# The last step of a Mamba scan on VectorE and ScalarE: states not stored, three factors multiplied at once

## What is computed

```python
def step(h, inp):                       # h: batch x 512 channels x 16 states
    d_t, u_t, B_t, C_t = inp
    dA = jnp.exp(d_t[..., None] * A)
    h = dA * h + (d_t * u_t)[..., None] * B_t[:, None, :]
    y = jnp.einsum('bdn,bn->bd', h, C_t)
    return (h, y)
_, ys = jax.lax.scan(step, h0, (deltas, us, Bs, Cs))
y = (ys + us * D[None, None, :]) * _silu(zs)
out = jnp.einsum('md,lbd->lbm', out_proj_w, y)
```

## Time and profile before

| what | us |
|---|---|
| runs: median (lowest to highest of 3) | 541.82 (541.18 to 544.04) |
| the profiled execution, its span | 540.9 |
| busy in the span: TensorE / VectorE / ScalarE / GpSimd | 437.8 / 399.3 / 314.3 / 216.1 |
| last scan step on VectorE, first product to last gate | 229.79 to 253.85 |
| first attention projection starts | 255.05 |

### The profile page before, as it was taken

One profiled execution on the slowest core, in us unless ns is written; L12 is line 12 of the kernel. 1 busy time (PEld: TensorE's weight loads), 2 busy tenths in 40 slices (PEclk: granted clock), 3 DMA queues, 4 the chain that ended last, 5 costly groups with the idle time before them and its releaser, 6 DMA issues.

```text
span 540.9 us, 9798 instructions
## 1 busy us (share of the span) xinstructions
PE 437.8 (81%) x3248; PEld 360.2 (67%) x3248; DVE 399.3 (74%) x734; ACT 314.3 (58%) x728; POOL 216.1 (40%) x157
## 2 busy tenths in 40 slices
PE   4979931848688685868999999999999999998733
PEld 1435621727577474756888988888988888897512
DVE  1867699796999999996564677776767777677453
ACT  2646995686999988986143453534355353435310
POOL 2300009793978979780323222223222223323010
PEclk9989975787896979889999999999999999999865
DMA  8952538031110223123000000000000000000000
GB/s 291 362 221 79 161 99 268 26 92 47 50 39 21 70 67 118 53 74 123 19 1 1 11 2 21 0 0 19 0 19 0 19 0 0 19 0 21 0 10 10
DMA packets 18795, 32.92 MB, mean 61 GB/s; under 512 B 2129, under 2 KB 11729, under 8 KB 17937
## 3 DMA queue, kind: packets, MB, share of 16 engines
q1 hardware_dynamic: 18768, 32.59, 18.1%
HBM read 26.26 MB, written 6.32 MB: 60 GB/s over the span
## 4 chain that ended last, share of the span: by engine, by line
PE 40%; issue 19%; ACT 15%; DVE 14%; DMA 6%; POOL 4%; SPq 1%; DVEq 0%; POOLq 0%; ACTq 0%
PE ps L398 32%; PE ps L505 5%; DMA ud_t<-ud_dram 4%; ACT hc L831 4%; ACT ps L823 2%; DVE reg_b L1227 2%; POOL reg_b L1056 2%; PE ps L602 2%; ACT reg_b L806 2%; ACT reg_b L918 1%; POOL small L1038 1%; DVE ps L1220 1%; DVE reg_b L1118 1%; DVE reg_b L1280 1%; DMA Nw<-x_fm 1%
## 5 line engine op out<-in xcount | busy, mean ns | idle before, releaser
L1033 POOL TENSOR_TENSOR reg_b<-reg_c,reg_a 128x1024 f32<-128x1024 f32 x56 | 130.5, 2372 | 60.7 <-DVE reg_c L1170 60.4
L1056 POOL TENSOR_TENSOR reg_b<-reg_b 128x768 f32<-128x768 f32 x32 | 58.0, 1812 | 140.1 <-DVE reg_b L1280 107.5
L398 PE MATMUL ps<-x1T,Mw 128*128 (+1 forms) x768 | 93.6, 278 | 0.6 <-ACT Mw L884 0.6
L831 ACT ACTIVATE hc<-reg_b,bc 128x512 f32<-128x512 f32 x112 | 79.8, 713 | 21.6 <-PE ps L505 18.3
L398 PEld LDWEIGHTS ps<-x1T,Mw 128*128 128x128 f32 x768 | 88.2, 192 | 4.3 <-ACT Mw L884 0.9
L505 PE MATMUL ps<-ident,hc 128*128 128x128 f32 x452 | 75.9, 318 | 15.3 <-ACT hc L831 15.1
L1227 DVE SCALAR_TENSOR_TENSOR reg_b<-reg_c,bc,ps 128x512 f32<-128x512 f32 x112 | 81.9, 736 | 0.0
L505 PEld LDWEIGHTS ps<-ident,hc 128*128 128x128 f32 x452 | 62.0, 165 | 26.2 <-ACT hc L831 25.1
L1220 DVE TENSOR_TENSOR ps<-ps,reg_b 128x512 f32<-128x512 f32 x96 | 65.8, 690 | 7.6 <-ACT ps L823 7.5
L823 ACT ACTIVATE ps<-reg_b 128x512 f32<-128x512 f32 x112 | 65.5, 586 | 4.1 <-POOL reg_b L1033 4.1
L918 ACT ACTIVATE reg_b<-ps,small 128x128 f32<-128x128 f32 x128 | 45.3, 366 | 38.8 <-DVE small L1285 38.2
(11 more groups left out here) (138 smaller groups left out, 705.8 us busy)
## 6 DMA issues: line engine op xcount, KB each, us to landing
reg_a<-a_dram SPq DMA_DIRECT2D x4, 1024.0 KB, 8.0
Mw<-w_o SPq DMA_DIRECT2D x1, 2048.0 KB, 15.9
ud_dram<-reg_b SPq DMA_DIRECT2D x4, 512.0 KB, 3.8
zs_dram<-x1T SPq DMA_DIRECT2D x4, 512.0 KB, 3.7
mring<-w_q SPq DMA_DIRECT2D x8, 256.0 KB, 2.9
ud_t<-ud_dram SPq DMA_DIRECT2D x8, 256.0 KB, 3.3
zs_t<-zs_dram SPq DMA_DIRECT2D x8, 256.0 KB, 2.7
Nw<-zeros SPq DMA_DIRECT2D x1, 2048.0 KB, 9.8
```

The costliest lines, as they stand in the source:

```text
L398: return pe.matmul(o, l, r, start=start, stop=stop)
L831: act.activation(hc[:, (n + 1) % WRING, :], H[:, n, :], ACT.Copy, scale=bc[:, t, s:s + 1]).then_inc(hc_s, 1)
L1033: pool.tensor_tensor(dA[:, g % RING], delta_r[:, bass.ds(t, 1), :].to_broadcast([P, SA, DI]), Abc[:, g * SA:(g + 1) * SA, :], ALU.mult).th ...
L1056: pool.tensor_tensor(rq[:, g % 2].rearrange("p a c n -> p (a c n)"), pc[:, g % 2].rearrange("p a c n -> p (a c n)"), psn[:, g % 2].rearran ...
```

## The change

In step 7 no state is stored, since no later step reads one. As y is the sum over n of C * (dA * h + B * du), it is split: the sum of C*B is one scalar per row (cb_last, made in the first part), and du times that scalar is added to ud_t, so that it comes onto Y with the skip row; what is left of each state is dA * C * h, one VectorE instruction that reads the exponential in PSUM, C as a scalar and the old state, and writes hc. ScalarE weighs nothing in step 7. The step is written out as `last_step`: it first waits for ud_t's load. The loop runs over steps 2 to 6. In `last_step` gate(6) stands after state 3, norm1_stats(6) after state 10 and norm1(6) after state 13. Two semaphores are new: udl_s (ud_t is complete) and yl_s (a product is written), and the sum takes small[:, 18:19]. The diff without the declarations:

```diff
--- before.py
+++ after.py
@@ -508,14 +508,17 @@
             def skip_sum(t):
 
                 need(pe, y2_s, t)
-                pe.wait_ge(st_u, 16 * (t + 1))
+                if t == T - 1:
+                    pe.wait_ge(udl_s, 1)
+                else:
+                    pe.wait_ge(st_u, 16 * (t + 1))
                 for c in range(CI):
                     last = turn_onto(Y[:, c * P:(c + 1) * P], ud_t[:, c * P:(c + 1) * P], c == 0, False)
                 last.then_inc(udm, 1)
 
-            def state_sum(slot, count, last_state):
-
-                pe.wait_ge(hc_s, count)
+            def state_sum(slot, done, count, last_state):
+
+                pe.wait_ge(done, count)
                 for c in range(CI):
                     last = turn_onto(Y[:, c * P:(c + 1) * P], hc[:, slot, c * P:(c + 1) * P], False, last_state)
                 last.then_inc(y_s, 1)
@@ -539,12 +542,15 @@
                 last.then_inc(x1Tm, 1)
 
             skip_sum(0)
-            state_sum(0, 1, True)
+            state_sum(0, hc_s, 1, True)
             pe.wait_ge(ld["wout"], 16)
             for t in range(1, T):
                 skip_sum(t)
                 for n in range(NST):
-                    state_sum((n + 1) % WRING, NST * (t - 1) + n + 2, n == NST - 1)
+                    if t == T - 1:
+                        state_sum((n + 1) % WRING, yl_s, n + 1, n == NST - 1)
+                    else:
+                        state_sum((n + 1) % WRING, hc_s, NST * (t - 1) + n + 2, n == NST - 1)
                     if n in PE_SIDE:
                         side_job(per_step * (t - 1) + PE_SIDE.index(n))
                     if n == 3:
@@ -815,7 +821,10 @@
 
 
                 act.wait_ge(arg_s, AG * (t - 1) + n // SA + 1)
-                need(act, h_s, NST * (t - 1) + n + 1 - RING)
+                if t == T - 1 and n >= RING:
+                    act.wait_ge(yl_s, n + 1 - RING)
+                else:
+                    need(act, h_s, NST * (t - 1) + n + 1 - RING)
                 if t == 1 and n == 0:
                     act.wait_ge(act_free, freed[("Z", CI - 1)][1])
                 if t == 1 and n == 2:
@@ -888,9 +897,9 @@
             def scan_step(t, carried):
                 for n in range(NST):
                     decay(t, n)
-                    if n >= BEHIND:
+                    if n >= BEHIND and t < T - 1:
                         weigh(t, n - BEHIND)
-                    elif carried:
+                    elif n < BEHIND and carried:
                         weigh(t - 1, NST + n - BEHIND)
                     if n in ACT_SIDE:
                         take_side(per_step * (t - 1) + ACT_SIDE.index(n))
@@ -900,8 +909,6 @@
 
             for t in range(1, T):
                 scan_step(t, t > 1)
-            for n in range(BEHIND):
-                weigh(T - 1, NST + n - BEHIND)
             for j in range(len(side) - sum(n >= NST for n in ACT_SIDE), len(side)):
                 take_side(j)
             take_x1(T - 1)
@@ -1194,7 +1201,11 @@
             softplus(1)
             dve.wait_ge(cb_s, 1)
             dve.tensor_reduce(cb0, cb_n[:, :], AX.X, ALU.add).then_inc(cb_s, 1)
+            dve.wait_ge(cb_s, 2)
+            dve.tensor_tensor(cb_n[:, :], bc[:, T - 1, 0:NST], bc[:, T - 1, NST:2 * NST], ALU.mult).then_inc(cb_s, 1)
             step_inputs(0)
+            dve.wait_ge(cb_s, 3)
+            dve.tensor_reduce(cb_last, cb_n[:, :], AX.X, ALU.add).then_inc(cb_s, 1)
             softplus(2)
             step_inputs(1)
             softplus(3)
@@ -1268,9 +1279,30 @@
                     elif n == 11:
                         norm1(t - 1)
 
+            def last_step():
+
+                t = T - 1
+                dve.wait_ge(st_u, 16 * T)
+                dve.wait_ge(cb_s, 4)
+                dve.scalar_tensor_tensor(ud_t[:, :], du_r[:, t, :], cb_last, ud_t[:, :], ALU.mult,
+                                         ALU.add).then_inc(udl_s, 1)
+                for n in range(NST):
+                    dve.wait_ge(da_s, NST * (t - 1) + n + 1)
+                    dve.wait_ge(y_s, NST * (t - 1) + n + 2 - WRING)
+                    dve.scalar_tensor_tensor(hc[:, (n + 1) % WRING, :], ps[:, n % RING, :],
+                                             bc[:, t, NST + n:NST + n + 1], H[:, n, :], ALU.mult,
+                                             ALU.mult).then_inc(yl_s, 1)
+                    if n == 3:
+                        gate(t - 1)
+                    elif n == 10:
+                        norm1_stats(t - 1)
+                    elif n == 13:
+                        norm1(t - 1)
+
             scan_step(1)
-            with dve.Fori(2, T) as t:
+            with dve.Fori(2, T - 1) as t:
                 scan_step(t)
+            last_step()
 
             def rope(k, g):
                 dve.wait_ge(xa_s, k + 1)
```

More of the change, by code:

```diff
@@ L123, in decoder_layer @@
         stats2, aggr2 = small[:, 48:54], small[:, 54:56]
-        cb0 = small[:, 62:63]
+        cb0, cb_last = small[:, 62:63], small[:, 18:19]
         spare = small[:, 63:64]
@@ L211, in decoder_layer @@
         arg_s = sem("arg_s"); da_s = sem("da_s"); dah_s = sem("dah_s"); h_s = sem("h_s")
-        cb_s = sem("cb_s"); hc_s = sem("hc_s"); y_s = sem("y_s"); udm = sem("udm")
+        cb_s = sem("cb_s"); hc_s = sem("hc_s"); yl_s = sem("yl_s"); udl_s = sem("udl_s"); y_s = sem("y_s"); udm = sem("udm")
         st_x = sem("st_x"); st_z = sem("st_z"); st_u = sem("st_u")
```

## The result

| kernel | median, us | lowest to highest | ratio to before (95% interval) |
|---|---|---|---|
| before | 541.82 | 541.0 to 544.04 (5 runs) | |
| changed | 545.49 | 544.55 to 546.17 (5 runs) | 1.0061 (1.0041 to 1.0081) |
| changed, once more beside the later experiments | 545.54 | 543.66 to 547.07 (12 runs) | 1.0059 (1.0038 to 1.0081) |

Times in us are read from medians; whether a kernel is faster or slower is read from the ratio.

The account below looks back on a forecast made before the run. The prediction took step 7's end to hang on ud_t's late load, then TensorE up to the first attention projection. +3.96 (gate) + 0.59 (clock) - 1.38 (lighter VectorE) = +3.2 us, from 541.82 to 545.0, range 542.3 to 546.8.

Parts of the forecast that it names:

- The wait at the head: Start of step 7: VectorE stands about 7.5 us until ud_t lands; ScalarE stands too after four exponentials.
- The gate behind it: Step 7: gate(6) follows ud_t's wait and four states, so TensorE starts the skip sum 3.96 us later.
- The slow clock: Skip sum to state 4 on TensorE: 6.42 us instead of 5.83 after longer idle time, +0.59 us.
- step 2's row: Same piece, skip sum to state 4, in scan step 2 before the change: 6.42 us after 8.51 us idle.
- The tail: State 4 to the last side job in step 7: 9.1 us against 10.48 with lighter VectorE work, -1.38 us.
- A state's price: Step 7 on VectorE: the one remaining instruction per state costs 0.65 us of queue, bounds 0.605 and 0.736.
- The beginning: First part, between the softplus parts: two small added instructions fall into VectorE's waits and cost nothing; uncovered, about 0.3 us.
- Behind the scan: After step 7: the rope tables' load goes out later, with 6.7 us left before use; costed at nothing.
- What bounds the kernel before: Step 7: ud_t's late load, then TensorE up to the first attention projection at 255.05; VectorE's queue alone doesn't decide.
- TensorE alone in the tail: Rival, from state 4 on: norm1(6) is ready in time, tail 7.5 us, total +1.6 or +1.0; chance 0.17.
- second slow stretch: Rival, before turn_x1(6): TensorE's new idle time slows its clock again, total +4.5 us, 546.3; chance 0.12.
- VectorE's queue as the limit: Rival, step 7: VectorE's queue and not the gate's place decides, -2.9 us, 538.9; chance 0.05.

Follow-up runs that it names:

- wait-only kernel: Kernel before with step 7 written out behind the loop on VectorE and a wait for ud_t's load at its head, arithmetic unchanged: 547.75 us, ratio 1.0102.
- The experiment with the gate first: Changed kernel with gate(6) moved to the head of last_step, ahead of the wait for ud_t: 541.92 us, ratio to before 1.000.
- kept-busy run: Changed kernel with 64 unused transposes of ident on TensorE ahead of skip_sum(7): 543.58 us, ratio to before 1.0027.

## Why the prediction was right, point by point

Forecast 545.0, measured 545.49; the sum was +3.2, the medians differ by 3.7 and the traces by 3.20 at the first projection, counted from ud_t's issue (in the profile's own time it starts at 256.35 and not at 258.2, because the issue itself came 1.90 sooner). The mechanism was right as well, in the order forecast. That the sum and the traces agree so closely is luck, since the terms are off by up to 0.18 us and cancel; of the 0.5 by which the medians go beyond the traces, 0.2 lies outside the span and the rest stays open.

- *The wait at the head.* VectorE idle 7.5 us expected, 7.21 seen; in the wait-only kernel 7.31. ScalarE did stand behind it, for 6.22 us, as said.
- *The gate behind it.* +3.96 expected, +3.78 seen; ud_t came 0.26 us quicker after its issue (3.34 us to VectorE's first instruction, 3.60 to TensorE's in the earlier trace rows), and the addition, four states and the gate took 4.04 instead of 3.96. TensorE's idle time 8.26 for 8.44. The experiment with the gate first shows that the gate's place behind the wait is the cause of the loss.
- *The slow clock.* +0.59 expected from step 2's row, +0.66 seen. It is the least certain term, and that it came so near is luck: the same kernel gave 5.98 instead of 6.49 in its second profile. Step 2's row was taken since its idle time was nearest, and this ground doesn't hold: by the table above 3.29 us idle led to 7.06, beyond the bound of 6.71 that I gave, and 10.53 to 6.12. The Trainium skill (TensorE: Matmul & The Clock Gate, Part 1) says that activity releases the throttle of an idle array. The kept-busy run agrees with it: the clock was 1.00 from 234 to 245.
- *The tail.* -1.38 expected, -1.24 seen (9.24 for 9.1). The wait for x1 was 1.11 for 1.3, and norm1's place its cause.
- *A state's price.* 0.65 us of queue expected for the new instruction: four take 2.72 at a duration of 0.75 each, that is 0.66 between starts.
- *The beginning.* Nothing expected. From the reduction of cb_n to the instruction that waits for ScalarE it is 5.40 us in both kernels (59.25 to 64.65, 61.22 to 66.62 in the earlier trace rows): the two instructions lie inside the waits. *Behind the scan.* The tables had the 6.7 us foreseen (252.69 to 259.40), and the wait ahead of L1311 was TensorE's, as before.
- *What bounds the kernel before.* The prediction followed TensorE from ud_t on and said that VectorE's queue alone doesn't tell when the step ends. The two experiments on the kernel before show that it does, but for 0.45 us: 23.61 us from first product to last gate, whether ud_t comes early or is waited for at the head, against 24.06. This didn't hurt the sum: its terms started from measured stretches, and that VectorE's queue makes TensorE's tail of 10.48 longer than it need be was reckoned with in the last of them.
- *Not foreseen.* GpSimd, of which I said that it runs ahead and isn't late, was itself stopped for 2.99 us by the exponentials; nobody waited for it. And the kernel before with the wait alone was expected at +7.5 and came at +6.3 by the medians, +6.8 in the trace: I counted all of the wait, though 0.45 us of it is made good behind it in this step. The 0.5 between the trace and the medians stays open.

Of the rivals, TensorE alone in the tail was refuted by the wait of 1.11 us; no second slow stretch came (the clock was 1.00 from 244 on). VectorE's queue as the limit is refuted for the changed kernel, where VectorE waits for TensorE, and shown for the kernel before, where the earlier transfer brought nothing measurable. The Trainium skill (Perfetto Trace Analysis, Identifying the Most-Contended Engine) says to optimize the engine of the highest occupancy first. That was VectorE, busy for 21.96 of the 24 us from 230 to 254. Here the rule was right and not enough: with 8 us of VectorE's work gone the kernel got slower, since the same edit put a foreign wait at the head of its queue. With the wait gone, the relief counted (4.9 us).

## What to carry to other kernels

When an edit lets a busy engine take over a little work that needs a transfer, look at what else stands behind that instruction in its queue, and at who waits for it: put the steps that others wait for ahead of the new wait, or issue the transfer before the wait that holds its queue. Two edits that bring nothing or a loss alone can bring 1% together; so cost a lighter queue together with every wait that the same edit puts into it. And the order within an engine's queue has a price of its own (here norm1 two states later: 0.85 us).

## What the runs showed of the hardware

With sixty-four transposes of no use the kernel's median was 2.0 us lower (543.58 against 545.54, intervals that overlap a little). The traces show a cause: after 8.26 us without work TensorE ran the 20 transposes and the start of the out projection at a granted clock of 0.50, and the piece took 5.98 to 6.49 us; kept at work, or starting within 1.31 us of other work, it took 4.19 at 1.00 in all three traces. I had reckoned with a gain, but with 4.2 as its far end; it came out exactly there.

The clock fell elsewhere too, without a long idle time. In step 6 of the same kept-busy kernel TensorE waited for ScalarE between states, 0.84 us at the longest, and its granted clock was 0.50 from 230 to 232, where the second profile of the changed kernel had 0.50 from 229 to 231 and the first profile 1.00 from 226 to 232. That is a spread from one execution to the next that the change has no part in.
